# A two-layer transformer kernel on one core: scores behind a step's first products, four row sets for turned maxima, and a first block whose feed-forward input comes in two steps

## The reference, cut to what matters

```python
# first layer ("first block" below), for each of 8 sequences
h  = layer_norm(x, g1, b1) * (1 + scale) + shift          # scale, shift from the condition
s  = q @ k.T / 4 - torus_dist * torus_scale[head]         # 512 x 512, 16 heads
x  = x + (softmax(s) @ v) @ Wout
x  = x + gelu_tanh(layer_norm(x, g2, b2) @ W1 + b1) @ W2 + b2
# second layer ("second block"), for each of 8 sequences
s  = where(node_mask, q @ k.T / 4, -inf)                  # masked keys
x  = x + gate1 * modulate(layer_norm(softmax(s) @ v @ proj_w + proj_b), shift1, scale1)
x  = x + gate2 * modulate(layer_norm(gelu(x @ fc1_w + b) @ fc2_w + b), shift2, scale2)
```

## Time and profile before

| | |
|---|---|
| median of the runs | 1400.09 us |
| profiled execution | 1405.66 us (its span 1403.9 us) |
| TensorE busy | 1294.1 us, 92% |
| VectorE / ScalarE / GpSimd busy | 803.9 / 744.4 / 757.0 us |
| first block, 100 to 800 us | TensorE busy 96 to 98 of each 100 us |
| second block, 884 to 1350 us | 466 us, TensorE busy about 421 |
| mean granted TensorE clock | 0.982 |

### The profile page before, as it was taken

One profiled execution on the slowest core, in us unless ns is written; L12 is line 12 of the kernel. 1 busy time (PEld: TensorE's weight loads), 2 busy tenths in 40 slices (PEclk: granted clock), 3 DMA queues, 4 the chain that ended last, 5 costly groups with the idle time before them and its releaser, 6 DMA issues.

```text
span 1403.9 us, 24536 instructions
## 1 busy us (share of the span) xinstructions
PE 1294.1 (92%) x8789; PEld 994.4 (71%) x8789; DVE 803.9 (57%) x2240; ACT 744.4 (53%) x1246; POOL 757.0 (54%) x939
## 2 busy tenths in 40 slices
PE   4899999999999999999999998889898989989777
PEld 3577778778778777777778777667666656666656
DVE  3766845746746746746745743565646546564552
ACT  3466765765665665765765663434444444444432
POOL 3698867867877867867867861110403222240323
PEclk9899999999999999999999998999999999999998
DMA  8532332332322322322322324443334242433100
GB/s 259 143 101 74 74 102 54 78 97 54 84 91 54 84 90 54 93 82 54 95 80 76 101 74 122 150 126 135 125 111 165 60 150 77 147 105 118 46 2 30
DMA packets 98259, 133.98 MB, mean 95 GB/s; under 512 B 16802, under 2 KB 51498, under 8 KB 98130
## 3 DMA queue, kind: packets, MB, share of 16 engines
q1 hardware_dynamic: 96850, 131.80, 31.8%
q10 hardware_dynamic: 1280, 0.53, 0.1%
HBM read 72.64 MB, written 58.75 MB: 94 GB/s over the span
## 4 chain that ended last, share of the span: by engine, by line
PE 68%; DVE 19%; issue 4%; DMA 3%; ACT 3%; POOL 2%; SPq 1%; DVEq 0%; POOLq 0%; ACTq 0%
PE dense L777 17%; PE dense L797 15%; PE turned L881 11%; PE pv L896 7%; DVE shifted L1401 6%; PE score L869 6%; DVE x_norm L1241 3%; PE turned L938 2%; PE score L919 2%; PE pv L948 2%; DMA q_rows<-peaks 2%; DVE feat_m L1358 2%; PE dense L785 1%; POOL shifted L631 1%; ACT probs L1112 1%
## 5 line engine op out<-in xcount | busy, mean ns | idle before, releaser
L1401 DVE CUSTOM_DVE_ANT_0 shifted<-score,bias 128x512 f32<-128x512 f32 x512 | 332.1, 686 | 260.3 <-PE score L869 138.7
L631 POOL TENSOR_SCALAR shifted<-shifted,row_max 128x512 f32<-128x512 f32 x512 | 361.1, 718 | 199.8 <-DVE row_max L1401 198.1
L1112 ACT ACTIVATE probs<-turned 128x512 f32<-128x512 f32 x512 | 277.9, 595 | 222.7 <-PE turned L881 222.2
L881 PE MATMUL turned<-ident,shifted 128*128 128x128 f32 x2048 | 270.0, 275 | 6.5 <-POOL shifted L631 6.0
L881 PEld LDWEIGHTS turned<-ident,shifted 128*128 128x128 f32 x2048 | 232.4, 141 | 59.6 <-issue 28.9
L797 PE MATMUL dense<-w_down,hidden 128*128 128x256 f32 x1024 | 258.2, 383 | 0.8 <-ACT hidden L1093 0.8
L624 POOL TENSOR_SCALAR bias<-dist,scale 128x1024 f32<-128x1024 f32 x192 | 218.4, 1138 | 13.8 <-DMA down_bias<-in_L_cond_b 13.8
L869 PE MATMUL score<-k_rows,q_rows 97*128 97x512 f32 x512 | 202.5, 458 | 13.9 <-DMA k_rows<-mask_neg 4.4
L797 PEld LDWEIGHTS dense<-w_down,hidden 128*128 128x128 f32 x1024 | 181.0, 191 | 33.3 <-issue 9.6
L777 PE MATMUL dense<-feat_m,w_up 128*128 128x512 f32 x768 | 188.3, 399 | 1.6 <-DVE feat_m L1358 1.6
L777 PEld LDWEIGHTS dense<-feat_m,w_up 128*128 128x128 f32 x768 | 144.6, 191 | 32.4 <-issue 2.0
(11 more groups left out here) (138 smaller groups left out, 1475.6 us busy)
## 6 DMA issues: line engine op xcount, KB each, us to landing
qk_rows<-qk_high SPq DMA_DIRECT2D x128, 256.0 KB
q_rows<-qk_rows SPq DMA_DIRECT2D x64, 384.0 KB
qk_rows<-qk_low SPq DMA_DIRECT2D x64, 256.0 KB
k_rows<-qk_rows SPq DMA_DIRECT2D x68, 192.0 KB
x_in_t<-in_x SPq DMA_DIRECT2D x8, 512.0 KB, 4.8
x_res<-in_x SPq DMA_DIRECT2D x8, 512.0 KB, 5.7
x_mid<-x_norm SPq DMA_DIRECT2D x8, 512.0 KB, 3.3
x_in_t<-x_mid SPq DMA_DIRECT2D x8, 512.0 KB, 4.0
```

What stands on the lines that cost most here:

```text
L631: ins = pool.tensor_scalar(shifted[:, u % 3, i, :], shifted[:, u % 3, i, :], -1.0, row_max[:, t % 6:t % 6 + 1], ALU.mult, ALU.add)
L881: mm = pe.transpose(turned_bank[z % 2][:, HALF * kk + P * i:HALF * kk + P * i + P], shifted[:, u % 3, i, P * kt:P * kt + P], ident[:, :])
L1112: act.activation(probs[:, u % RING, 2 * pair:2 * pair + 2, :], turned_bank[z % 2][:, :].rearrange("p (a c) -> p a c", a=2), ACT.Exp)\
L1401: dve.tensor_tensor_reduce(shifted[:, u % 3, i, :], score_bank[t % 2], bias[:, u % 2, i, :], 1.0, 3.0e38, ALU.add, ALU.min, row_max[:, t % ...
```

## The change

**Second block.** The pair scores move from the head of a step to behind slot 3p (its products and its `down` chunks), before slot 3p+1. `peaks` becomes four row sets, which lie in the unused tile `no_bias`, with one semaphore each: `take_peaks` waits for the load of four pairs before. The slots 3p get work: `up` 0 and `up` 4 move one slot ahead (9 and 12), and `down` chunks are laid out anew. There is a 14th step, in which the last chunk of a pass is issued (slot 39), behind the last division.

**First block.** `t2` is spread over steps 15 and 16; the `up` products, the fourth `qk` and the first `down` chunks come one step later. The sums of the norm of sequence n+2 are taken in step 34, in the tail of pass n, instead of in step 4 of pass n+1 (pass 0 keeps them in step 4 too, for sequence 1). GpSimd's `inverse_std` moves ahead of the first subtraction of a pass.

```diff
 FIRST:
-             12: [("qk", 0)], 13: [("qk", 1)], 14: [("qk", 2)], 15: [("t2", 0), ("t2", 1)],
-             17: [("up", 0), ("up", 1), ("up", 2), ("up", 3)], 18: [("qk", 3)],
-             20: [("up", 4), ("up", 5), ("up", 6), ("up", 7)],
-             24: [("down", 0)], 28: ...
-    AMID = (17, 20)
+             12: [("qk", 0)], 13: [("qk", 1)], 14: [("qk", 2)], 15: [("t2", 0)], 16: [("t2", 1)],
+             18: [("up", 0), ("up", 1), ("up", 2), ("up", 3)], 19: [("qk", 3)],
+             21: [("up", 4), ("up", 5), ("up", 6), ("up", 7)],
+             25: [("down", 0)], 28: ...
+    AMID = (18, 21)
-    FIRST_DOWN = {21: (0, 3), 22: (3, 5), 23: (5, 6), 24: (6, 9), 25: (9, 12), 26: (12, 14), 27: (14, 15), 28: (15, 18),
-                  29: (18, 20), 30: (20, 22), ...
-    FIRST_NORM = {4: ("stats", 0), 6: ("norm", 0), 11: ("stats", 1), 13: ("norm", 1)}
-    ADD_BIAS = {17: 0, 18: 1, 20: 2, 21: 3}
+    FIRST_DOWN = {22: (0, 3), 23: (3, 4), 24: (4, 7), 25: (7, 10), 26: (10, 13), 27: (13, 14), 28: (14, 17), 29: (17, 20),
+                  30: (20, 22), ...
+    FIRST_NORM = {4: ("stats", 1), 6: ("norm", 1), 11: ("stats", -1), 13: ("norm", -1), 34: ("stats", 2)}
+    ADD_BIAS = {18: 0, 19: 1, 21: 2, 22: 3}
 HEADS:
-             10: [("up", 0), ("up", 1), ("up", 2), ("up", 3)], 13: [("up", 4), ("up", 5), ("up", 6), ("up", 7)],
-             19: [("down", 0)], 23: [("down", 1)], 29: [("down", 2)], 38: [("down", 3)]}
-    HEAD_STEPS = H // 2 + 5
-    HEADS_DOWN = {16: (0, 5), 17: (5, 6), 19: (6, 9), 20: (9, 10), 22: (10, 15), 23: (15, 16), 25: (16, 18), 26: (18, 19),
-                  28: (19, 23), 29: (23, 24), 31: (24, 26), 32: (26, 27), 35: (27, 30), 38: (30, 32)}
+             9: [("up", 0)], 10: [("up", 1), ("up", 2), ("up", 3)], 12: [("up", 4)], 13: [("up", 5), ("up", 6), ("up", 7)],
+             19: [("down", 0)], 23: [("down", 1)], 29: [("down", 2)], 39: [("down", 3)]}
+    HEAD_STEPS = H // 2 + 6
+    HEADS_DOWN = {15: (0, 1), 16: (1, 6), 18: (6, 7), 19: (7, 9), 20: (9, 10), 21: (10, 11), 22: (11, 15), 23: (15, 16),
+                  24: (16, 17), 25: (17, 18), 26: (18, 19), 27: (19, 20), 28: (20, 23), 29: (23, 24), 31: (24, 26),
+                  32: (26, 27), 35: (27, 29), 38: (29, 31), 39: (31, 32)}
-        peaks = sb("peaks", [4 * TT, P], F32R)
+        peaks = no_bias[0:4 * TT, :].rearrange("p (i q) -> p i q", q=P)
 GpSimd, turn(n) of the first block:
+                    if 0 < n < B - 1:
+                        inverse_std(n + 1, 0)
                     for k in range(UNITS):
                         subtract_max(n, k)
                         ...
-                        if k == 4 and n + 1 < B:
-                            inverse_std(n + 1, 0)
+                        if k == 4 and n == 0:
+                            inverse_std(1, 0)
 TensorE, turned_scores_of and turn(n) of the second block:
-                pe.wait_ge(s["peaks_loaded"], 16 * (H // 2 * (n - B) + q + 1))
+                pe.wait_ge(s[f"peaks_loaded{q % 4}"], 16 * (H // 8 * (n - B) + q // 4 + 1))
-                        if 2 <= p < 2 + H // 2:
-                            pair_scores_of(n, p - 2)
                         for k in range(3 * p, 3 * p + 2):
+                            if k == 3 * p + 1 and 2 <= p < 2 + H // 2:
+                                pair_scores_of(n, p - 2)
 VectorE, take_peaks:
-                if count > 0:
-                    dve.wait_ge(s["peaks_loaded"], 16 * count)
-                dve.tensor_scalar(peaks[:, :], score_bank[0][0:4 * TT, 0:P], -1.0, None, ALU.mult)\
+                if count > 3:
+                    dve.wait_ge(s[f"peaks_loaded{q % 4}"], 16 * (count // 4))
+                dve.tensor_scalar(peaks[:, q % 4, :].bitcast(F32R), score_bank[0][0:4 * TT, 0:P], -1.0, None, ALU.mult)\
```

More of the change, by code:

```diff
@@ L55, in build @@
              5: [("wout", 0)], 6: [("wout", 1)], 8: [("t1", 0), ("wout", 2)], 9: [("t1", 1)], 10: [("wout", 3)],
[3 rows of a table removed]
-             24: [("down", 0)], 28: [("down", 1)], 31: [("down", 2)], 35: [("down", 3)]}
-    AMID = (17, 20)
[3 rows of a table added]
+             25: [("down", 0)], 28: [("down", 1)], 31: [("down", 2)], 35: [("down", 3)]}
+    AMID = (18, 21)
     AHEAD = {33: 0, 35: 1}
     STEPS = UNITS + 5
-    FIRST_DOWN = {21: (0, 3), 22: (3, 5), 23: (5, 6), 24: (6, 9), 25: (9, 12), 26: (12, 14), 27: (14, 15), 28: (15, 18),
-                  29: (18, 20), 30: (20, 22), 31: (22, 24), 32: (24, 27), 33: (27, 28), 34: (28, 30), 35: (30, 32)}
-    FIRST_NORM = {4: ("stats", 0), 6: ("norm", 0), 11: ("stats", 1), 13: ("norm", 1)}
-    ADD_BIAS = {17: 0, 18: 1, 20: 2, 21: 3}
+    FIRST_DOWN = {22: (0, 3), 23: (3, 4), 24: (4, 7), 25: (7, 10), 26: (10, 13), 27: (13, 14), 28: (14, 17), 29: (17, 20),
+                  30: (20, 22), 31: (22, 24), 32: (24, 27), 33: (27, 28), 34: (28, 30), 35: (30, 32)}
+    FIRST_NORM = {4: ("stats", 1), 6: ("norm", 1), 11: ("stats", -1), 13: ("norm", -1), 34: ("stats", 2)}
+    ADD_BIAS = {18: 0, 19: 1, 21: 2, 22: 3}
     HEADS = {0: [("v", 3), ("t1", 0), ("t3", 0), ("t3", 1)], 1: [("t1", 1)], 2: [("wout", 0), ("wout", 1)],
@@ L991, in turn @@
                     for p in range(HEAD_STEPS):
-                        attended = p >= 6 and p % 2 == 0
-                        if 2 <= p < 2 + H // 2:
-                            pair_scores_of(n, p - 2)
+                        attended = 6 <= p < 6 + 2 * G and p % 2 == 0
                         for k in range(3 * p, 3 * p + 2):
+                            if k == 3 * p + 1 and 2 <= p < 2 + H // 2:
+                                pair_scores_of(n, p - 2)
                             for piece, m in pieces(HEADS, k, n):
@@ L1133, in load_peaks @@
                 act.wait_ge(s["peaks_ready"], H // 2 * (n - B) + q + 1)
-                act.dma_start(q_rows[PEAK_AT:ALL_ROWS, g, pair, :].bitcast(F32), peaks[:, :].bitcast(F32))\
-                    .then_inc(s["peaks_loaded"], 16)
+                act.dma_start(q_rows[PEAK_AT:ALL_ROWS, g, pair, :].bitcast(F32), peaks[:, q % 4, :])\
+                    .then_inc(s[f"peaks_loaded{q % 4}"], 16)
             def normalize(m):
@@ L1174, in turn @@
                             normalize(n - 2)
-                        if p >= 6 and p % 2 == 0:
+                        if 6 <= p < 6 + 2 * G and p % 2 == 0:
                             take_heads_out(n, (p - 6) // 2)
@@ L1553, in turn @@
                     if n < B and k in FIRST_NORM:
-                        what, i = FIRST_NORM[k]
-                        m = n + 1 if i == 0 else n - 1
-                        if 0 <= m < B:
-                            first_norm(what, i, m)
+                        what, ahead = FIRST_NORM[k]
+                        if 0 <= n + ahead < B and not (what == "stats" and ahead == 1 and n > 0):
+                            first_norm(what, 1 if ahead < 0 else 0, n + ahead)
                     if n >= B and k in ANY_NORM:
```

2 lines of the change are left out of this document (1 added, 1 removed).

## The result

The changed kernel takes 1375.88 us, the median of 4 runs (1374.59 to 1377.58); the kernel before took 1399.88 us in 4 runs beside it (1396.74 to 1400.62). The ratio is 0.9824, 95% interval 0.9805 to 0.9843: 24.0 us faster. The forecast was 1373.6 us with a range of 1362 to 1390. The profiled execution took 1377.58 us (span 1375.7), against 1405.66 us (span 1403.9) before: 28.1 us less by the profiles, against the predicted sum of 26.6.

A forecast was written before the change was run, and what follows sets the result against it. TensorE's list was taken to set the time in both blocks, so only its waits could be won. 8.6 - 1.0 + 11.6 + 3.0 + 2.6 + 1.8 = 26.6 us off 1405.66 gave 1379.1, scaled 1373.6 us; range 1362 to 1390.

The forecast's parts named there:

- Part 1, the short waits: Second block, pair scores waiting for VectorE's peaks, three short waits a pass: moving the scores wins 8.6 us, less 1.0.
- The waits of steps 4 and 5: Second block, scores' waits of 0.46 and 0.37 us: both go, 0.83 us a pass.
- That of step 3: Second block, scores' wait of 1.11 us: 0.25 us won a pass, ends 0 and 1.11, as `up` 0 needs `t2`'s low parts.
- the chain of 1.0 us: Second block, step 9, scores to the maxima's transpose with one chunk less cover: net 0.13 us lost in 8 passes.
- Part 2, four row sets: Second block, step 6, passes 10 to 14: long waits (9.1 us) and slow clock (3.3) go, less 0.8: 11.6 us.
- the residual: Pass 12, turned scores of pair 2: landing took 7.3 us against 6.5 available, so 0.8 us of waiting remains.
- The first rival, the landing in the wait's place: Second block: TensorE waits for the load at the turned scores instead; sum 15.0 us, 1385 us; chance 0.16.
- The scaling: The sum was made against the profiled 1405.66 us; the result was scaled by 1400.09/1405.66 to the median, giving 1373.6 us.
- Part 3, the 14th step: Second block, first `t3` waiting for the last division: 0.25 us in six passes, 0.65 after pass 14, 0.8 at end: 3.0 us.
- Part 4, first block: Norm's sums in the tail win 0.44 us in six passes (2.6); `t2` in two steps 0.25 in seven (1.8).
- the first block loses: First block, short steps 16, 17, 20: -0.9 us in seven passes, 1 us in six tails; 1388 us; chance 0.12.
- The slower rival: Second block, steps 5 to 9: stretched casts of the maxima lose about 1.0 us each, 40 us: 1413 us; chance 0.04.

The follow-up runs named there:

- After with 13 steps: Kernel after with the last `down` chunk back in slot 38 and no 14th step: 1380.83 us, 0.9864 to the kernel before.
- four sets alone: Kernel before with only the four row sets for `peaks`: 1391.89 us, 0.9940.
- the second block alone: Kernel after with the first block of the kernel before: 1376.91 us, 0.9849 to the kernel before.
- `t2` in one step: Kernel after with first-block `t2`, `up`, `qk` and `down` as before, sums still in the tail: 1373.34 us; run again, 1373.81 us.
- The low parts ahead of the peaks: Kernel after with VectorE making the low parts of `t2` before the first pair's maxima, and TensorE's order changed to suit: 1375.18 us, 0.9826 to the kernel before.
- first block alone: Kernel before with only the first block's part of the change: 1396.77 us, 0.9976.
- scores moved: Kernel before with scores behind slot 3p, new `down` layout and 14 steps, but one `peaks` tile and the old first block: 1391.94 us, 0.9943.

## Why the prediction was right, and where it wasn't

**Part 1, the short waits: right in its mechanism, and near in size because two errors partly cancel.** Predicted were 8.6 - 1.0 = 7.6 us. After with 13 steps against four sets alone (both without long waits) differ in the table by 6.9 us, and by 8.5 if the 4.60 us of `w_out` are set to the 3.07 that it took in the other. The waits of steps 4 and 5 are gone: 0.83 us in eight passes, 6.6 us. That of step 3 only changed its place, 1.11 us before the scores to 1.12 before `up` 0, so its lower end, 0, was the right one, and the 2.0 us credited for it weren't won. The feared waits of the transpose for the split came to one of 0.22 us in the whole block, in the last pass; the chain of 1.0 us that was subtracted isn't seen apart from the rest. What the 6.9 to 8.5 us hold beyond the 6.6 isn't traced.

**Part 2, four row sets: right in its mechanism, the residual 0 and not 0.8 us.** From step 5 to step 7 passes 10 to 14 lose 12.2 us in the kernel before (8.9 us in five waits, and 1.64 us twice at the lower clock), and nothing in that with four sets alone. The first rival, the landing in the wait's place, didn't occur: no turned scores waited for the load, which has 6.73 us in the kernel after. Its 7.3 us against 6.5 were read from the worst of five landings. The five long ones of each of the three profiles of the old second block lie between 4.3 and 6.1 us but for this one.

**The scaling was wrong.** The sum was made against one execution, and scaled by 1400.09/1405.66 as if its surplus of 5.6 us lay in all work alike. It lay mostly in what the change removes: the long waits and the slow steps behind them, which vary from run to run. The profile that was read had 12.2 us of them; two profiles of the same second block, of executions at 1396.8 and 1397.9 us, had 8.2 and 8.9. Alone, the sets saved 15.1 us between the two profiled executions (16.1 over the eight passes), 10.8 and 11.7 us over the eight passes against those two other profiles, and 8.4 us (5.9 to 11.1) in the ratio. So the term of 11.6 us was true of one execution and some 3 us too large for the median. The profiles give 28.1 us for the whole change, the medians 24.0; the forecast sum was 26.6, and its 1373.6 came out 2.3 us too low. That the total came so near is in part luck: parts 1 and 4 each hold two errors of opposite sign. The runs themselves say the same: those of the kernel before spread from 1395.3 to 1407.5 us, those of the kernel after from 1373.7 to 1377.6.

**Part 3, the 14th step: right to within its error.** 3.0 us predicted; 2.4 and 4.4 us by the traces, about 5 by the medians. From pass 9 to 13 the first `t3` no longer waits, as predicted, and at the end its wait fell from 1.62 to 0.87 us. The step missed that the second `t1` then waits 0.63 us, for VectorE's additions behind the division. What was won at `w_out` (1.21 to 0.68 us) pays for most of it: 0.37 us a pass is left, where 0.25 was predicted. Parts 1 and 3 together were to give 10.6 us behind four sets; the second block alone takes 464.6 us over the eight passes, 10.5 less than with four sets alone.

**Part 4, first block: the sum 4.4 came out as 2.9; one term was too small, the other had the wrong sign.** From the norm in pass 0 to that in pass 6 five profiles with the old first block take 602.8 to 603.5 us (mean 603.2), three with the sums moved 599.3 in the mean, six with `t2` in two steps as well 600.4. So the sums gave 3.9 us and not 2.6, and `t2` in two steps cost 1.1 us and did not win 1.8. In passes 2 to 6 the sums gave 0.97 us a pass and not 0.44. "More does not [go]: VectorE's own chain ... over the 3.03 us of the norm ... sets the pace" took the norm's duration as fixed; it fell to 2.52 us. GpSimd's `inverse_std` no longer ran just ahead of it, and VectorE had 1.11 us of idle in the step before the norm where it had none; that the shorter norm comes from the GpSimd work beside it is likely and not isolated. Against it stand 0.2 us in pass 0, where the sums are taken twice, and the wait of 0.88 in pass 1, which were not in the sum. `t2` in two steps won nothing in any pass, where 0.25 us was predicted. The cause of the wait was right by the profile's own naming after the change, an exponential behind the activations of `t2`, but parting these moves the queue from one exponential to the next: the wait is 0.60 instead of 0.85 us, and the waits of the scores' weight loads for VectorE over passes 2 to 6 are 33 of 12.8 us, against 28 of 11.2 us with `t2` in one step. The rival "the first block loses" at -0.9 us a pass had the sign of this edit and far too high a price.

**The slower rival** would have needed 0.67 us a step from step 5 on. GpSimd's additions fall in steps 3 and 4, as argued; the one cast of a pass that was stretched, 0.74 us at 1058.62, was over long before it was needed: the split was ready at 1059.56 and TensorE came to its transpose at 1061.30, behind its `up` products. The low parts ahead of the peaks show what happens where that cover is thinner. (The prediction's "0.17 in the steps around" was misread: in the kernel before the cast of the next step, at 1138.23, was stretched too, to 0.79 us.)

## What to carry to other kernels

A wait for a single small buffer has two cures, another buffer or another order of the traffic in front of its load; here the first gave 8.4 us and the second 5.5, with intervals that overlap, and the second only moves the late landings to a place where nothing on TensorE waits for them. A sum from one profile has to be weighed term by term against the spread of the runs: a term made of waits on transfers belongs to that execution, a term that recurs to the hundredth in every pass belongs to the kernel. And a piece that is parted to shorten a queue must be followed to the next item of the same queue, before anything is credited for it.

## What the runs showed of the hardware

- A load of 8 KB issued by ScalarE was seen as landed after 7.3 us while SyncE had 512 KB transfers under way, after 5.8 us in the kernel with one set and moved scores. With these transfers moved behind, the tile was free again within 3.5 us (issued at 1141.20 in pass 12, written at 1144.74).
- The clock after one and the same idle differed between executions. Before `w_out` of pass 9, TensorE was idle for 2.13 and then 0.68 us in the kernel before and in that with 13 steps, and 2.12 and 0.68 us with four sets alone. The granted clock then was 0.70, 0.66 and 1.00, and the 24 products took 4.33, 4.60 and 3.07 us. The kernel after, profiled twice, had 2.98 us at 1.00 and 4.60 us at 0.66 (927.5 to 932.5) there, both behind 1.99 and 0.68 us of idle. The long waits at step 6 say the same: behind one of 1.70 us (first block alone, pass 11) the clock fell and step 6 took 6.03 us instead of 4.41; behind one of 2.01 us (scores moved, pass 11) it stayed at 1.00 and step 6 took its usual 4.30. A difference of 1.5 us between two profiles at such a place says nothing about an edit.
- In the last pass the kernel after had 0.62 and 0.60 over 13 us, behind 3.12 us of idle up to 1278.48 and 1.02 us up to 1282.53. Its second profile, behind 3.03 and 1.02 us, had 0.74 over the same 13 us, and 18 `up` products took 4.45 us there instead of 5.41. The first profile, then the second:
```profile
1277.00:1282.00 5.00, 2.81 (x9) 1.56 (x9) 4.90 (x12) 1.19 (x2) 1.68 (x3) 0.62 0.00 0
1282.00:1290.00 8.00, 7.47 (x23) 6.15 (x24) 2.18 (x5) 2.66 (x3) 4.42 (x2) 0.60 0.01 3
```
```profile
1277.00:1282.00 5.00, 2.67 (x9) 1.43 (x9) 4.90 (x12) 1.20 (x2) 1.53 (x3) 0.74 0.00 0
1282.00:1290.00 8.00, 7.63 (x28) 6.36 (x29) 2.04 (x5) 3.35 (x4) 4.57 (x2) 0.74 0.01 3
```
- A VectorE cast of 128x8 takes 0.17 us alone. Where it started while GpSimd ran an addition of 128x1024 it took 0.74, 0.79, 1.48 or 1.73 us, and it ended 0.02 to 0.03 us behind the addition each time (for example the cast of the earlier trace rows at 1134.05, and the addition, 2.42 us from 1131.61, at 1134.03): the cast's length is what was left of the addition.
- The same four VectorE norms of 128x256 took 2.52, 3.03 or 3.31 us. GpSimd ran subtractions and a bias beside all of them, in different parts; no run isolates what makes the difference.
